# A recommendation tower on one core: the grams of a block in a row, pairs read by twins of features, and the last half block sent through DRAM

## The reference

```python
e = jnp.stack([tbl_0[ids[:, 0]], tbl_1[ids[:, 1]], ...], axis=1)      # (2048, 27, 128)
x = einsum('bfd,bgd->bfg', e, e).reshape(B, F * F)[:, TRIL_IDX]        # the 351 with f > g
h = concatenate([r_bottom_mlp_out, x, r_bottom_mlp_out], axis=1)       # (2048, 607)
h = maximum(h @ W_top1 + b_top1, 0)                                    # 512
h = maximum(h @ W_top2 + b_top2, 0)                                    # 256
y = h @ W_top3
```

## Time and profile before

| | us |
|---|---|
| median of 3 runs | 407.44 |
| lowest and highest | 405.29, 408.83 |
| the profiled execution | 408.56 |
| its span | 406.8 |
| TensorE (PE) busy in it | 357.0 (88%) |
| GpSimd (POOL) | 250.9 (62%) |
| VectorE (DVE) | 220.1 (54%) |
| ScalarE (ACT) | 158.7 (39%) |
| DMA packets | 60681, 45.55 MB |

### The profile page before, as it was taken

One profiled execution on the slowest core, in us unless ns is written; L12 is line 12 of the kernel. 1 busy time (PEld: TensorE's weight loads), 2 busy tenths in 40 slices (PEclk: granted clock), 3 DMA queues, 4 the chain that ended last, 5 costly groups with the idle time before them and its releaser, 6 DMA issues.

```text
span 406.8 us, 9934 instructions
## 1 busy us (share of the span) xinstructions
PE 357.0 (88%) x3895; PEld 301.1 (74%) x3895; DVE 220.1 (54%) x524; ACT 158.7 (39%) x257; POOL 250.9 (62%) x247
## 2 busy tenths in 40 slices
PE   0770776789699999999999999999999999977997
PEld 0550654678588879889788889799688798876795
DVE  0760687784369984524298983233689835300400
ACT  2321243565224354453334354453243643621533
POOL 5777287677777777777775777777727776000000
PEclk9985799999989999999999999999999999988999
DMA  6999233482655552336454633355445523211100
GB/s 188 232 249 259 72 88 82 134 205 66 160 138 137 127 120 69 86 94 160 138 122 106 138 93 72 83 148 153 112 99 121 127 62 80 53 51 30 24 2 0
DMA packets 60681, 45.55 MB, mean 112 GB/s; under 512 B 31711, under 2 KB 51687, under 8 KB 60635
## 3 DMA queue, kind: packets, MB, share of 16 engines
q1 hardware_dynamic: 51332, 27.39, 28.2%
q0 software_dynamic: 7680, 15.74, 15.8%
q10 hardware_dynamic: 1623, 1.79, 1.8%
HBM read 40.03 MB, written 4.85 MB: 110 GB/s over the span
## 4 chain that ended last, share of the span: by engine, by line
PE 75%; DMA 6%; SPq 6%; DVE 6%; ACT 4%; issue 2%; ACTq 0%
PE ps_build L735 38%; PE ps_dense L782 10%; PE ps_gram L759 9%; PE ps_dense L811 7%; DMA id_raw<-ids_onehot_dram 4%; SPq L296 3%; PE ps_gram L744 3%; ACT embT L569 2%; DVE table L434 2%; PE ps_dense L819 2%; DMA gram_dram<-gram 2%; PE ps_build L744 2%; DVE hot L457 1%; ACT table L558 1%; SPq L297 1%
## 5 line engine op out<-in xcount | busy, mean ns | idle before, releaser
L417 POOL DMA_INDIRECT rows<-tbl_dram,idx x240 | 250.1, 1042 | 92.1 <-issue 69.2
L735 PE MATMUL ps_build<-hot,table 125*128 125x512 f32 x768 | 191.2, 404 | 35.7 <-DVE hot L457 35.1
L735 PEld LDWEIGHTS ps_build<-hot,table 125*128 125x128 f32 x768 | 144.1, 193 | 73.4 <-issue 29.0
L457 DVE TENSOR_SCALAR hot<-id_raw 125x512 fp32r<-125x512 f32 x384 | 154.0, 443 | 55.3 <-PE ps_build L735 51.1
L569 ACT COPY embT<-ps_build 128x512 f32<-128x512 f32 x48 | 57.9, 1207 | 141.3 <-PE ps_build L735 136.2
L759 PE MATMUL ps_gram<-embT 128*53 128x52 f32 x1792 | 48.5, 217 | 4.7 <-DVE gram L465 3.9
L759 PEld LDWEIGHTS ps_gram<-embT 128*53 128x53 f32 x1792 | 46.8, 132 | 7.0 <-issue 5.4
L465 DVE COPY gram<-ps_gram 117x416 f32<-117x416 f32 x28 | 15.5, 587 | 37.6 <-DMA gram_dram<-gram 23.0
L782 PE MATMUL ps_dense<-pairT,w1p 120*128 120x256 f32 (+1 forms) x252 | 35.6, 288 | 0.0
L448 DVE TENSOR_SCALAR id_raw<-id_raw,vocab 125x512 f32<-125x512 int32 x48 | 23.4, 488 | 18.3 <-DMA id_raw<-ids_onehot_dram 18.3
L782 PEld LDWEIGHTS ps_dense<-pairT,w1p 120*128 120x128 f32 (+1 forms) x252 | 33.1, 197 | 0.0
(11 more groups left out here) (61 smaller groups left out, 131.4 us busy)
## 6 DMA issues: line engine op xcount, KB each, us to landing
id_raw<-ids_onehot_dram SPq DMA_DIRECT2D x144, 64.0 KB
raw<-tbl_dram SPq DMA_DIRECT2D x12, 448.0 KB
gram_dram<-gram SPq DMA_DIRECT2D x56, 84.5 KB
rows<-tbl_dram,idx POOLq DMA_INDIRECT x240
id_raw<-ids_onehot_dram SPq DMA_DIRECT2D x12, 256.0 KB
bot<-bottom_dram SPq DMA_DIRECT2D x7, 128.0 KB, 2.4
w1p_raw<-w_pairs_dram ACTq DMA_DIRECT2D x1, 720.0 KB
raw<-tbl_dram SPq DMA_DIRECT2D x12, 52.0 KB
```

The costliest lines, as they stand in the source:

```text
L417: nc.gpsimd.indirect_dma_start(rows[:, t % 2, s * D:(s + 1) * D], None, tables[f], bass.IndirectOffsetOnAxis(idx[:, TILES * i + t, f:f + 1 ...
L457: nc.vector.tensor_scalar(hot[0:VP, a % HOT_SLOTS, :], shifted, float(v), None, ALU.is_equal).then_inc(hot_made, 1)
L735: last = nc.tensor.matmul(bank[:, :], table[0:VP, n, bits, v * D:(v + 1) * D], hot[0:VP, a % HOT_SLOTS, :], start=(v == bits == 0), stop=( ...
```

## The change

- **Order.** Both transposes `("rows", 3, 0)` and `("rows", 3, 1)` now stand before gram 0; then gram 0, gram 1, the other two transposes, gram 2, gram 3, and after them all layers of the second half. ScalarE's high parts of that half move from behind `("rows", 3, 2)` to behind `("three", 0)`, VectorE's low parts from behind gram 0 to behind the block's last hot.
- **Twins.** The scratch in DRAM is laid out by twins of features: (gram, 13 twins, 26 rows, 2, 32 samples). A row of `gram` that went out as one run of 26 x 32 numbers goes out as 13 runs of 2 x 32. Rows of two neighbouring features then lie one behind the other, and a half's pairs take 18 reads of up to 50 partitions in place of 29 of up to 26; the runs read are 32 numbers long as before. The weights' rows are put in the new order of pairs on the host, and the chunks of pairs are cut at 111 and 229 instead of 120 and 231.
- **SP's queue.** `pace` is gone. The ids of a table and block come in one DMA of 512 columns in place of four of 128. After half of the first half's reads come the ids of table 3, after the rest those of tables 4 to 11. The next block's first three tables' ids come ahead of the four writes, not between them.
- **The end.** `end_products`, `relayout`, `pairs_back` and what belongs to them are gone. All four grams of the last block are made by `pair_products`, go to DRAM and come back. Grams 1 and 3 are copied to a second tile, `last_gram`, and both halves' pairs, vectors and results have buffers of their own in the space of `table`, which is free after the block's last hot. SP writes grams 0 and 1, reads the first half's pairs, writes grams 2 and 3, reads the second half's. On ScalarE the casts of the first half's pairs follow the copies of gram 3 and stand ahead of the activations of `("one", 1, 0)`; VectorE does both parts of the second half. The layers run by `last_order`, in the six banks of the builds and grams.

```diff
-CHUNK_AT = (0, 120, 231, 351)
+TWINS = PG // 2
+CHUNK_AT = (0, 111, 229, 351)
...
+def pair_order():
+
+    pairs = [(2 * q + 1, 2 * q + 2) for q in range(TWINS)]
+    for q in range(TWINS):
+        pairs += [(r, 2 * q + n + 1) for r in range(2 * q + 1) for n in range(2)]
+    return pairs
...
+    reads = [(0, 0, TWINS, (3, first + 4))]
+    at = TWINS
+    for q in range(TWINS):
+        n = 2 * (2 * q + 1)
+        cuts = {17: (0, 16, n), 19: (0, 16, n), 21: (0, 16, n), 23: (0, 32, n)}.get(n // 2, (0, n))
...
+            reads.append((c, at - CHUNK_AT[c], b - a, (q * first + a, 1)))
...
              ("hot", 10), ("two", 0), ("rows", 2, 2), ("rows", 2, 3), ("hot", 11), ("three", 0), ("rows", 3, 0),
-             ("gram", 0), ("rows", 3, 1), ("rows", 3, 2), ("gram", 1), ("rows", 3, 3), ("one", 1, 0), ("gram", 2),
-             ("one", 1, 1), ("gram", 3), ("two", 1), ("three", 1)]
+             ("rows", 3, 1),
+             ("gram", 0), ("gram", 1), ("rows", 3, 2), ("rows", 3, 3), ("gram", 2), ("gram", 3), ("one", 1, 0),
+             ("one", 1, 1), ("two", 1), ("three", 1)]
+    last_order = order[:order.index(("gram", 3)) + 1] + [
+        ("one", 1, 0), ("one", 1, 1), ("last1", 0, 0), ("two", 1), ("last1", 0, 1), ("three", 1), ("last2", 0), ("last3", 0),
+        ("last1", 1, 0), ("last1", 1, 1), ("last2", 1), ("last3", 1)]
...
+        last_gram = over("last_gram", [GM, DUO, PG, JT], fp32, table_at)
+        last_pairT = [over(f"last_pairT{l}", [CHUNK, 2, 3, HALF], fp32r, table_at + (8 + 6 * l) * KIB) for l in range(2)]
+        last_pairX = [over(f"last_pairX{l}", [CHUNK, 3, HALF], fp32, table_at + (11 + 6 * l) * KIB) for l in range(2)]
...
+        def gram_free(engine, i, t):
+
+            if is_at(i, LAST) and t == 1:
+                engine.wait_ge(built, BUILDS * LAST + nth("hot", NO - 1) + 1)
+            elif is_at(i, LAST) and t > 1:
+                engine.wait_ge(last_gram_out if t % 2 else gram_out, TILE_OUT * (1 if t % 2 else TILES * i + 1))
+            elif not (is_at(i, FIRST) and t == 0):
+                engine.wait_ge(gram_out, TILE_OUT * (TILES * i + t))
 
         def build_at(s):
...
-            def load_id_piece(i, n, p):
-
-                if p == 0:
-                    ids_free(i, n)
-                src = ids_onehot[n:n + 1, i * BLOCK + p * PIECE:i * BLOCK + (p + 1) * PIECE]
-                dst = id_raw[:, n % ID_SLOTS, p * PIECE:(p + 1) * PIECE]
-                sp.dma_start(dst, src.broadcast_to([128, PIECE])).then_inc(id_in[n % ID_SLOTS], 16)
-
-            def pace(i, g):
-
-                if g < (TILES - 1) * NG or i < LAST:
-                    sp.wait_ge(gather_sent, NG * (TILES * i + 1) + g + 1)
...
+            def next_ids(i, n):
 
                 h, m = (i, n - ID_SLOTS) if n >= ID_SLOTS else (i - 1, [m for m in range(NO) if m % ID_SLOTS == n][-1])
                 sp.wait_ge(hot_made, HOTS * h + VB * (m + 1))
                 sp.sem_inc(loads_begun, 1)
+                load_ids(i, n)
...
                 for k in range(GROUP):
                     row = k // DUO * STRIP + k % DUO * FEATURES
-                    src = gram[row:row + PG, k % DUO, :, :].rearrange("p n j -> p (n j)")
-                    sp.dma_start(scratch[t * GROUP + k, :, :, :].rearrange("r n j -> r (n j)"), src).then_inc(gram_out, 16)
+                    src = gram[row:row + PG, k % DUO, :, :].rearrange("p (q n) j -> p q (n j)", n=2)
+                    signal = last_gram_out if is_at(i, LAST) and t % 2 else gram_out
+                    sp.dma_start(scratch[t * GROUP + k, :, :, :, :].rearrange("q r n j -> r q (n j)"),
+                                 src).then_inc(signal, 16)
...
+            def read_pairs(half, s, dst=pairX, signals=pairs_in):
+
+                src = scratch[half * 2 * GROUP:(half + 1) * 2 * GROUP, :, :, :, :].rearrange("g q r n j -> (q r n) g j")
+                c, p, count, (a, step) = reads[s]
+                rows = src[a:a + (count - 1) * step + 1:step] if step > 1 else src[a:a + count]
+                sp.dma_start(dst[p:p + count, c, :].rearrange("p (g j) -> p g j", j=JT), rows).then_inc(signals[c], 16)
...
-                for s in range(READS):
-                    pace(i, 7 * s // 8)
+                for s in range(READS // 2):
                     read_pairs(0, s)
-                    load_id_piece(i, *later[s])
-                for n, p in later[READS:]:
-                    load_id_piece(i, n, p)
+                next_ids(i, ID_SLOTS)
+                for s in range(READS // 2, READS):
+                    read_pairs(0, s)
+                for n in range(ID_SLOTS + 1, NO):
+                    next_ids(i, n)
                 load_bottom(b, at - HALF)
                 pairs_written(i - 1, 1)
                 for s in range(READS):
-                    pace(i, 34 + 4 * s // 7)
                     read_pairs(1, s)
...
-                for t in range(TILES if more else 2):
-                    write_gram(i, t)
-                    if more and t < ID_SLOTS:
-                        for p in range(PIECES):
-                            load_id_piece(i + 1, t, p)
...
+                next_ids(0, n)
+            for i in range(BLOCKS):
+                if i > FIRST:
+                    one_block(i, i * BLOCK)
+                if i < LAST:
+                    for n in range(ID_SLOTS):
+                        next_ids(i + 1, n)
+                    for t in range(TILES):
+                        write_gram(i, t)
+                    if i > FIRST:
+                        store(2 * i - 1, i * BLOCK - HALF)
             sp.wait_ge(built, BUILDS * LAST + nth("hot", NO - 1) + 1)
             sp.sem_inc(loads_begun, 1)
-            sp.dma_start(end_bot[:, :], bottom[:, END * HALF:(END + 1) * HALF]).then_inc(end_bot_in, 16)
-            load_bottom(END - 1, (END - 1) * HALF)
+            load_last(0)
+            load_last(1)
+            write_gram(LAST, 0)
+            write_gram(LAST, 1)
             pairs_written(LAST, 0)
             for s in range(READS):
-                read_pairs(0, s)
-            store(END - 2, (END - 2) * HALF)
-            sp.wait_ge(end_act, M2 + 1)
-            sp.sem_inc(loads_begun, 1)
-            sp.dma_start(out[END * HALF:(END + 1) * HALF, :].rearrange("b o -> o b"), end_y[:, :]).then_inc(out_done, 16)
-            store(END - 1, (END - 1) * HALF)
-            sp.wait_ge(out_done, 16 * (END + 1))
+                read_pairs(0, s, last_pairX[0], last_pairs_in[0])
+            write_gram(LAST, 2)
+            write_gram(LAST, 3)
+            pairs_written(LAST, 1)
+            for s in range(READS):
+                read_pairs(1, s, last_pairX[1], last_pairs_in[1])
+            store(2 * LAST - 1, LAST * BLOCK - HALF)
...
-                if i > FIRST:
-                    bottom_low(2 * i - 1)
-                    pairs_low(2 * i - 1)
                 empty_gram(i, 1)
...
+                    if a == HOTS - 1:
+                        bottom_low(2 * i - 1)
+                        pairs_low(2 * i - 1)
...
             hots(LAST)
-            empty_gram(LAST, 0)
-            bottom_low(2 * LAST - 1)
-            pairs_low(2 * LAST - 1)
-            empty_gram(LAST, 1)
...
-                for dst, src in pack_pieces(u):
-                    last = nc.vector.tensor_copy(dst, src)
-                last.then_inc(pack_dve, 1)
+            for t in range(TILES):
+                empty_gram(LAST, t)
+            dve.wait_ge(last_high, 2)
+            for l in range(2):
...
+                dve.wait_ge(last_high, c + 3)
+                low_part(last_pairT[0][0:n, LOW, c, :], last_pairX[0][0:n, c, :],
+                         last_pairT[0][0:n, HIGH, c, :]).then_inc(last_pair_low, 1)
...
-                        if dense and use[1:] in ((1, 1), (3, 2)):
-                            h = 2 * i - 2 + use[1] // 2
-                            bottom_high(h)
-                            pairs_high(h)
+                        if dense and use[1:] == (1, 1):
+                            bottom_high(2 * i - 2)
+                            pairs_high(2 * i - 2)
                     elif use[0] == "gram":
-                        if is_at(i, LAST) and use[1] >= 2:
-                            empty_end(use[1] - 2)
-                        else:
-                            empty_gram(i, use[1])
+                        empty_gram(i, use[1])
+                        if is_at(i, LAST) and use[1] == 1:
+                            for l in range(2):
+                                act.wait_ge(last_bot_in[l], 16)
+                                nc.scalar.copy(last_botT[l][:, HIGH, :], last_bot[l][:, :]).then_inc(last_high, 1)
+                        if is_at(i, LAST) and use[1] == 3:
+                            for c in range(3):
+                                n = CHUNKS[c]
+                                act.wait_ge(last_pairs_in[0][c], 16 * CHUNK_READS[c])
```

(19 more changed lines are left out.)

332 lines of the change are left out of this document (128 added, 204 removed).

## The result

| | us |
|---|---|
| before, median of 4 runs beside it | 408.13 |
| after, median of 4 runs (lowest, highest) | 439.69 (434.07, 441.13) |
| ratio, 95% interval | 1.0712, 1.0546 to 1.0878 |
| the profiled execution of after, its span | 441.06, 439.1 |

The account below looks back on a forecast made before the run. TensorE, busy 88% of a 406.8 us span, was taken as the bound. Blocks 2 and 3 +9.4, block 1 0, the end -5.0 summed to +4.4, so 411.8 us from a 407.44 median; range 403.5 to 420.

Parts of the forecast that it names:

- rule of divisors: Gram writes: a DMA uses the largest divisor up to 16 as engines, 13 for 26 rows: +0.9 us, not +0.7.
- Blocks 2 and 3: Grams in a row leave TensorE gaps: 3.9 us a block plus 0.8 for lower clock, together +9.4 us.
- X: Wait from one gram's last copy to the next gram's first: 4.6 us in blocks, 3.9 in the last.
- the base: X before the cost of small pieces: taken as 3.9 us, halfway between 3.25 without traffic and 4.5.
- X - 3.1: Blocks 2 and 3: TensorE's gap before gram 2, 1.5 us expected.
- X - 2.2: Blocks 2 and 3: TensorE's gap before gram 3, 2.4 us expected.
- The write: Gram writes in 256 B pieces: 24 ns each, 32.4 us engine time, +0.7 us, between -0.2 and +1.7.
- rival 1: Small writes cost nothing: X 3.4, together -6.3, 401 us; at X 3.9, 404.6 us; chance 0.25.
- Block 1: First block already has these waits; TensorE leaves grams sooner but waits for hots: 0.
- Reads and ids: SP's queue: 18 reads for 29, one id DMA for four, about 58 issues fewer a block; costed at nothing.
- Rival 3: Unpaced reads crowd gathers or ids; TensorE waits some 2 us early in three blocks: 418 us; chance 0.05.
- The end: Last block: faster grams, no turning round, less slow clock, against an activation wait of 3.6 us: -5.0 us.

Follow-up runs that it names:

- row_pieces: row with the gram writes cut into 256 B pieces, still 29 reads: 420.10 us, ratio 1.0258 to the kernel before.
- row: end_only with a block's grams in a row and ids between the writes: 415.68 us, ratio 1.0143 to the kernel before.
- ids_between: Changed kernel with CHUNK = 128 and the next block's first id loads between the gram writes, not ahead: 419.20 us, ratio 1.0274.
- end_only: Kernel before with only the last half block through DRAM, casts behind the layer-1 activations: 406.16 us, ratio 0.9916.
- b_w122: Kernel before with CHUNK, the partitions of the pairs' weight tiles, 122 instead of 120: 422.76 us, ratio 1.0383.
- cast_late: ids_between with the last block's first-half pair casts moved behind that half's layer-1 activations: 414.71 us, ratio 1.0175.

## Why the forecast was wrong, step by step

**The step that is missing: the chunk.** No step of the prediction priced the new cuts at 111 and 229. They raise the longest chunk from 120 to 122 and with it the partitions of a tile that is loaded while TensorE has no work in reserve: it waits some 1 us for each table's hots. The prediction put the start at nothing, without a word on it. 18.1 us of the 27.9 between the forecast sum and the profiled one stand at this place, 15.7 of them the stop, and the constant alone is worth 12.2 us in the one kernel and 14.8 in the other. The prediction had cited the very rule of divisors for the grams' writes, where it was worth 0.2 us a write, and had not put it to the one load whose partition count changed. The profile of before does not show such a stop (the issues behind the load of the pairs' weight were 0.45 and 0.94 us), but it does show what a stop would hit: ScalarE's copies and casts for the hots come right behind these issues in its order.

**Blocks 2 and 3: the mechanism held, X did not.** Two gaps before grams 2 and 3, lower clock behind them, all hidden work gone: as forecast. The sum had +9.4, the profile has +14.4, or 15.6 for the same work. The term that was mis-sized is the first X. The prediction lowered the base from 4.5 to 3.9 because no id loads would stand between the writes any more. They stand ahead of the first one, close together, and it lands 7.5 us after its first issue: X is 7.6, not 4.6. X - 3.1 gives a gap of 4.5, and 4.86 was measured; the second gap, forecast as X - 2.2 = 3.1 for the X of 5.3, is only 1.31, because the slow gram ahead of it (5.06 for 3.29) had taken 1.8 of it. Moving the ids back between the writes brings the stages to +4.8 and +4.4 (0.6 more each for the same work), and the forecast had +4.7 each. So the 9.4 us were about right for a kernel that this one is not; the runs on either side give 9.2 and 9.5 for the order.

**The write.** 0.7 us were taken, between -0.2 and +1.7. `row_pieces` shows 0.2 in X and nothing in the stages: nearer to rival 1. A write's engine time, put at 32.4 us or 24 ns a piece, is 26.0 us or 19 ns a piece, against 21.0 and 22.1 us of whole rows; it is a fifth more and not half as much again. But that rival ended at a faster kernel because it put X at 3.4 with no pieces to pay. X was 4.7 in `row` with none. What sets X in a block is not the pieces; the decisive number was the base, which the trace of before gave as 4.5 and the prediction talked down. That its X of 4.6 is what `row` and `ids_between` show (4.7 in the mean in both) is luck: a base 0.8 too low and a price of the pieces some 0.5 too high largely cancel.

**Block 1.** 0 was forecast, +3.0 is in the profile. `end_only`, which differs from before only in the last block, has 83.5 us there against 81.0, with gaps of 2.41 and 3.4 where the earlier trace rows has 1.01 and 2.91. `b_w122` has 80.0. This stage alone moves by 2 us and more from kernel to kernel with nothing changed in it, so how much of the 3.0 is the change is open; only the 0.6 of the moved transposes and the 0.92 behind late ids can be named.

**Reads and ids.** Costed at nothing, and that held for the third and the last block (+0.3 and +0.2, the moved transposes included). Rival 3 has its time from 2 us a block of waiting for ids. With 18 reads that mechanism is there in the second block alone: VectorE waits 1.17 and 1.08 us, TensorE 0.92. With 29 it is there in each, and costs 5.5 to 5.9 us in the last two. The prediction gave the reason wrongly: it looked at the share of the DMA engines (0.53), while what runs out is SP's queue, at some 0.4 us an issue.

**The end.** Forecast -5.0, measured -3.8. The wait for the activation was 4.70 (3.6 forecast), and the two pieces of layer 1 behind it, 405.96 to 411.17, took 5.2 us where the two ahead of it took 3.1 (398.12 to 401.25): 2.1 where 1.4 was forecast. Together 1.8 us more, and -3.2 us is what the end fell by for the same work; the other 0.6 are the transposes that moved out of the stage. The mechanism, casts ahead of the activation in ScalarE's order, is shown by `cast_late`. The second half's reads were done in time, as forecast: the last low part is made at 419, and TensorE wants it at 426.7.
